# A windowed-attention and expert layer on one core: clearing buffers later, router weights earlier, and the last chunk of rows in another order

## The chip, the core and the metric

The kernel runs on one core of a Trainium2 chip. The metric is device time in microseconds (us), lower is better. The core's engines are TensorE (PE, matrix products, whose weight loads are shown apart as PEld), VectorE (DVE), ScalarE (ACT), GpSimd (POOL) and SyncE (SP). SyncE here only issues DMA transfers. Each engine has its own instruction stream in program order, and they meet at semaphores.

## The reference

The input x is 8 sequences of 512 tokens with 256 channels, in float32. All that follows is float32.

```
xn   = layernorm(x)                                  # per token, eps 1e-5
qkv  = xn @ qkv_w.T                                  # 32 heads of 8
att  = q.k * 8**-0.5 * (8 - |i-j|/2)/8               # only for i-8 <= j < i+8
s    = softmax(att) @ v @ proj_w.T + proj_b
e    = argmax(xn @ router_w), score = sigmoid(max)   # 8 experts, one for each token
f    = (silu(xe @ gate_w[e]) * (xe @ up_w[e])) @ down_w[e]     # xe = xn * score
f   += (silu(xn @ shared_gate_w) * (xn @ shared_up_w)) @ shared_down_w
out  = x + s * silu(f)
```

## The kernel before, in words

The 4096 tokens are 32 tiles `t` of 128. X holds all of x, and later the normalised rows, then rows scaled for the experts, then the attention's result. xnT holds the normalised x transposed, with zero columns at both ends of each sequence. Attention goes by 64 units `n` of 2 blocks of 32 queries. A unit runs over several turns of one main loop, `for n in range(LAST + 1)` with LAST = 66, that each engine has in its own stream:

- PE: `scores(n)` from the block-diagonal key buffer kBD and the query buffer qBD (two of each, taken in turn for each half sequence), then `weighted(n - 2)`, the probabilities times the values in VB, and `output(t)` ("pr"), the projection of a finished tile.
- VectorE: `weigh` (scores times the distance weights into Sx), `largest`, `flipped` (32x32 transposes of the exponentials into PTs), `invert`, `divide`, `turned` (for the normalised output O and OT).
- GpSimd: `banded` (a mask, in some turns) and `subtract`; ACT: `exps`.

Ahead of the loop: SP issues the loads of x in five groups (`GROUPS`: tiles 0 to 3, 4 to 11, 12 to 19, 20 to 27, 28 to 31), and behind the first group those of two sets of constants and of the weights of q, k and v. VectorE takes the moments of group 0 (`moments(0)`, one instruction for each tile), forms mean and deviation in small operations on 128x4 (`variance`, `deviation`, with a square root on ACT), and normalises tiles 0 to 3 (`normalise(0)`; each second tile raises the semaphore `n_xn` by 1). PE transposes them and forms q, two sets of keys and the values of sequence 0. VectorE goes on with the moments of the other 28 tiles, then writes ones into two columns of each part of VB, and waits for the scores of unit 0. Meanwhile GpSimd clears `blank`, the ends of xnT, both kBD, both VB and the three Sx, and makes two bfloat16 copies of constants, all in one run. The semaphore `s_zero` is raised after the ends of xnT (to 1) and after Sx (to 2); ACT's first copy into qBD, VectorE's ones and first `weigh`, and SP's main loop wait for 2. Router weights are the last 8 columns of the tile wqkv; PE's first product for values (`values(0)`) waits for them.

The feed-forward part: the shared expert's products are the jobs "sg", "su" (gate and up, for half of the hidden channels of a sequence) and "sd" (down, for two tiles). ACT copies an "sd" into `shared_rows`. The routed tokens are sorted by expert into DRAM, worked on in tiles between units 18 and 40 or so, and their results lie in `ys_dram`. For each chunk `c` of two tiles (16 chunks), GpSimd's `gather(c)` adds the routed rows to the shared rows by two indirect DMAs, ACT's `silu(c)` takes a tanh, VectorE's `silu(c)` makes f(1 + tanh), VectorE's `result(c)` multiplies 0.5 of that with the attention's result (which `attention(t)` has put into X with the bias added), and GpSimd's `add_out` stores it with addition onto out, where x was copied before. The last chunk is different: `result(15)` adds it to the two tiles of x in XR, and SP stores XR plainly.

All products but scores and weighted values share four PSUM banks psM, given out in turn in the order of the list ORDER, which `jobs_of(n)` fills. `jobs_of(64)` holds "sd" for the last chunk, at U - 3 (U = 64), and "pr" of tile 30; "pr" of tile 31 stands in turn 66. In turn 64 PE does `weighted(62)` first and then that "sd" and "pr".

Of the kernel before, what the change touches and what calls it, by code (L numbers as in the profile page):

```python
# [11 lines left out]
ALU = mybir.AluOpType  # L12
# [3 lines left out]
P = 128  # L16
BATCH, SEQ, C = 8, 512, 256
# [3 lines left out]
T = NTOK // P  # L21
# [7 lines left out]
QB = 32  # L29
# [28 lines left out]
CT = 2  # L58
# [92 lines left out]


def result_at(n):
    last = {NC - 2: U + 1, NC - 1: LAST}
    return [c for c in range(NC) if last.get(c, max(C_STEP + 2 + c * 4 // 3, 4 * c + 6)) == n]


# [4 lines left out]
def build(nc, x, wqkv_d, wproj_d, router_w, gate_w, up_w, down_w, sgate_w, sup_w, sdown_w,  # L162
# [3 lines left out]
    with ctx:  # L166
# [132 lines left out]
        @block.sync  # L299
        def _(sp):  # L300
            for i, (lo, hi) in enumerate(GROUPS):
                sp.dma_start(X[:, lo:hi, :], x_tiles[:, lo:hi, :]).then_inc(s_x[i], 16)
                if i == 0:
                    sp.dma_start(cst[:, :], const[:, 0:C_STAY]).then_inc(s_const, 16)
                    sp.dma_start(rcst[:, :], const[:, C_STAY:C_END]).then_inc(s_const, 16)
                    sp.dma_start(wqkv[:, :, 0:3 * C], wqkv_d.rearrange("(k p) f -> p k f", p=P)).then_inc(s_wq, 16)
            for dst, src in ((wsgu[:, :, 0:F], sgate_w), (wsgu[:, :, F:2 * F], sup_w), (wsdn[:, :, :], sdown_w)):
                sp.dma_start(dst, src.rearrange("(k p) f -> p k f", p=P)).then_inc(s_ws, 16)
            sp.dma_start(wqkv[:, :, 3 * C:], router_w.rearrange("(k p) f -> p k f", p=P)).then_inc(s_wr, 16)
            sp.dma_start(wp[:, :, :], wproj_d).then_inc(s_ws, 16)  # L310
            sp.wait_ge(s_zero, 1)
            v_rows = v_dram.rearrange("(b w) c -> w b c", b=BATCH)
            for lo, hi in ((0, WIN), (WIN + SEQ, PADW)):
                sp.dma_start(v_rows[lo:hi], blank[0:hi - lo, :].unsqueeze(1).broadcast_to([hi - lo, BATCH, C])).then_inc(s_pad, 16)
            sp.wait_ge(s_zero, 2)
            sp.wait_ge(s_one, 1)

            def fill(i):
                n_r = min(4, NT - 4 * i)
                sp.dma_start(xs_dram[i * 4 * P:(i * 4 + n_r) * P, :].rearrange("(p r) c -> p r c", r=n_r),  # L320
                             blank[:, :].unsqueeze(1).broadcast_to([P, n_r, C])).then_inc(s_fill, 16)

            def keep_v(b):
                sp.wait_ge(a_V, BT * (b + 1))
                at = b * PADW + WIN
                sp.dma_start(v_dram[at:at + SEQ, :].rearrange("(t p) c -> p t c", p=P), vS[b % 2][:, :, 0:C]).then_inc(x_vd[b % 2], 16)

            def spread_v(n):
                b = n // UB
                sp.wait_ge(x_vd[b % 2], 16 * (b // 2 + 1))  # L330
                if n == 0:
                    sp.wait_ge(s_pad, 16 * 2)
                if n >= 2:
                    sp.wait_ge(a_PV, n - 1)
                at = first_key(n)
                for h in range(HS):
                    sp.dma_start(VB[n % 2][QB * h:QB * h + QB, :, :, h, 1:1 + VQ].rearrange("p i k c -> p (i k) c"),
                                 v_dram[at:at + P, h * VQ:(h + 1) * VQ].rearrange("(a p) c -> p a c", p=QB)).then_inc(x_v[n % 2], 16)

            def expert(i):  # L340
                return sp.value_load(etabi[0:1, i:i + 1], min_val=0, max_val=E - 1)

            def load_weights(i):
                e = expert(i)
                if i >= 2:
                    full(sp, ("xb", i - 2))
                for w, c0 in ((gate_w, 0), (up_w, F)):
                    sp.dma_start(egu[:, i % 2, :, c0:c0 + F],
                                 w[bass.ds(e, 1)].rearrange("e (k p) f -> p (e k) f", p=P)).then_inc(b_wg[i % 2], 16)

            def load_down(i):
                e = expert(i)
                if i >= 2:
                    full(sp, ("xc", i - 2))
                sp.dma_start(edn[:, i % 2, :, :],
                             down_w[bass.ds(e, 1)].rearrange("e (k p) c -> p (e k) c", p=P)).then_inc(b_wd[i % 2], 16)

            def load_rows(i):
                if i >= 4:
                    full(sp, ("xa", i - 4))  # L360
                sp.dma_start(stage[:, i % 4, :], xs_dram[i * P:(i + 1) * P, :]).then_inc(b_in[i % 4], 16)

            def preset(k):
                rows = slice(k * NTOK // 8, min((k + 1) * NTOK // 8, NTOK - CT * P))
                sp.dma_start(out[rows, :], x[rows, :]).then_inc(d_pre, 16)

            for n in range(LAST + 1):
                if BATCH < n - 1 < U:
                    spread_v(n - 1)
                if ROUTE <= n < ROUTE + 8:  # L370
                    preset(n - ROUTE)
                if n == C_STEP:
                    full(sp, ("xc", NX - 1))
                    sp.dma_start(XR.rearrange("p (t c) -> p t c", t=CT), x_tiles[:, T - CT:T, :]).then_inc(d_x, 16)
                for i in range(2 * n - 4, 2 * n - 2):
                    if 0 <= i < 10:
                        fill(i)
                if n == E0 - 1:
                    for k in range(SENDS):
                        sp.wait_ge(r_scat[k], 16 * (T // SENDS))  # L380
                    sp.wait_ge(r_tab, 1)
                    sp.wait_ge(s_cast, 2)
                    for i in range(2):
                        load_rows(i)
                for i in pair_at(n + 1, 0):
                    if i >= 2:
                        load_rows(i)
                for i in pair_at(n, 1):
                    load_down(i)
                for i in pair_at(n, 0):  # L390
                    load_weights(i)
                if 0 <= n - 1 < BATCH:
                    keep_v(n - 1)
                if 0 <= n - 1 <= BATCH:
                    spread_v(n - 1)
            sp.wait_ge(d_pre, 16 * 8)
            sp.wait_ge(d_o, 1)
            sp.dma_start(out_v[:, T - CT:T, :], XR.rearrange("p (t c) -> p t c", t=CT)).then_inc(d_end, 16)
            sp.wait_ge(d_end, 16)
            for b in range(3):  # L400
                sp.wait_ge(d_st[b], 16 * len(range(b, NC - 1, 3)))

        @block.gpsimd
        def _(pool):
# [1 line left out]
            zero(blank[:, :], 0.0)  # L406
            zero(xnT[:, :, :, 0:WIN], 0.0)
            zero(xnT[:, :, :, WIN + SEQ:PADW], 0.0).then_inc(s_zero, 1)
            for i in range(2):
                zero(kBD[i][:, :, :, :], 0.0)  # L410
            for v in VB:
                zero(v[:, :, :, :, :], 0.0)
            for s in Sx:
# [197 lines left out]
        def _(dve):  # L611
# [98 lines left out]
            def weigh(n):  # L710
                dve.wait_ge(a_S, n + 1)
                if n == 0:
                    dve.wait_ge(s_zero, 2)
                if n >= 3:
                    dve.wait_ge(a_PT, n - 2)
                s = Sx[n % 3][:, :, :].rearrange("p (j g) k -> p j g k", j=KC)[:, :, :, 0:KW]
                tt(s, psS[:, :, 0:BW].rearrange("p j (g k) -> p j g k", k=KW),  # L717
                   mw.unsqueeze(1).unsqueeze(1).broadcast_to([P, 2, G, KW]), ALU.mult).then_inc(a_mul, 1)
# [85 lines left out]
            def result(c):  # L804
# [2 lines left out]
                dve.wait_ge(a_s, CT * c + CT)  # L807
                dve.wait_ge(d_w, c + 1)
                stt(s, shared_rows(t).rearrange("p t c -> p (t c)"), 0.5, s, ALU.mult, ALU.mult).then_inc(d_g, 1)
                if c == NC - 1:  # L810
                    dve.wait_ge(d_x, 16)
                    dve.wait_ge(d_g, c + 1)
                    tt(XR, s, XR, ALU.add).then_inc(d_o, 1)

            moments(0)
            variance(0)
# [1 line left out]
            normalise(0)  # L818
            for i in range(1, len(GROUPS)):
                moments(i)  # L820
            dve.wait_ge(s_zero, 2)
            for v in VB:
                for h in range(HS):
                    for c in (0, 2 * VW - 1):
                        ins = nc.vector.memset(v[QB * h:QB * h + QB, :, :, h, c:c + 1], 1.0)
            ins.then_inc(s_one, 1)
            for n in range(LAST + 1):
                if n < U:
# [35 lines left out]
                if n < BATCH:  # L864
                    logits(n)
                for job in jobs_of(n):
                    if job[0] == "pr":
                        attention(job[1])
                if n == ROUTE - 1:
                    choose()  # L870
                for c in result_at(n):
# [3 lines left out]
        def _(pe):  # L875
# [146 lines left out]
            for n in range(LAST + 1):  # L1022
# [12 lines left out]
                    expert_down(i)  # L1035
                for i in pair_at(n, 1)[:1]:
                    expert_up(i)
                if 0 <= n - 2 < U:
                    weighted(n - 2)
                for i in pair_at(n, 1)[1:]:  # L1040
# [1 line left out]
                for i in pair_at(n, 0)[:1]:  # L1042
                    expert_rows(i)
                for job in jobs_of(n):
                    if job[0] in ("sg", "su", "sd"):
                        shared(*job)
                for i in pair_at(n, 0)[1:]:
                    expert_rows(i)
# [43 lines left out]
```

## Time and profile before

| | |
|---|---|
| median of 3 runs | 595.69 us (592.25, 595.69, 595.95) |
| the profiled execution: its own time | 597.03 us |
| the profiled execution: span | 595.0 us |
| PE busy | 545.0 us (92%) |
| VectorE busy | 440.0 us (74%) |
| ACT, GpSimd busy | 240.7 us (40%), 253.8 us (43%) |
| mean granted clock of PE | 0.979 |

The span goes from the profiled execution's first to its last event; its own time is 2.03 us longer. PE's granted clock is given as a share of 2.4 GHz. Busy time of PE is that of pipelined products and says little about its peak; waits and the chain of work are read from the rows below.

### The profile page before, as it was taken

How to read it: one execution, taken by the hardware profiler on the slowest of the kernel's cores; microseconds unless marked ns; L12 is line 12 of the kernel's file. 1: busy time of each engine (PE TensorE's matmuls, PEld its weight loads, DVE VectorE, ACT ScalarE, POOL GpSimd, SP SyncE). 2: the span in 40 equal slices, each digit the busy share in tenths (PEclk: the TensorE clock that was granted, in tenths of full speed). 3: DMA queues.
4: the chain of work that ended last, by engine and by line, in shares of the span. 5: the costliest groups of instructions: out<-in, count | busy, mean ns of one | idle time of the engine just before them, and what ended most of it. 6: DMA issues, size and time to landing. Idle time of an engine off the chain costs nothing.

```text
span 595.0 us, 10334 instructions
## 1 busy us (share of the span) xinstructions
PE 545.0 (92%) x3302; PEld 472.2 (79%) x3302; DVE 440.0 (74%) x1030; ACT 240.7 (40%) x506; POOL 253.8 (43%) x187
## 2 busy tenths in 40 slices
PE   1989999979998999999999999999999999989773
PEld 1747789858876899988899988899888878876662
DVE  6776867898758566566656656655899999989993
ACT  1464454526553433433443442353434454343210
POOL 7122333128885322322422422222466876966442
PEclk9979999989998999999999999999999999999987
DMA  8624533215634667767566757644233755646423
GB/s 304 210 80 141 190 121 124 90 53 181 193 107 138 198 191 208 209 192 211 158 183 212 213 169 213 203 134 133 62 59 59 99 79 83 89 60 92 60 36 54
DMA packets 106618, 83.17 MB, mean 140 GB/s; under 512 B 42181, under 2 KB 104773, under 8 KB 106437
## 3 DMA queue, kind: packets, MB, share of 16 engines
q1 hardware_dynamic: 90724, 65.07, 37.5%
q0 software_dynamic: 10224, 12.33, 12.5%
q10 hardware_dynamic: 5616, 5.11, 2.5%
q8 instruction: 27, 0.44, 0.3%
q14 instruction: 27, 0.21, 0.1%
HBM read 59.41 MB, written 27.00 MB: 145 GB/s over the span
## 4 chain that ended last, share of the span: by engine, by line
PE 60%; DVE 15%; POOL 8%; issue 5%; ACT 5%; DMA 4%; SPq 1%; ACTq 0%; DVEq 0%
PE psM L1002 11%; PE psV L952 11%; PE psS L927 8%; PE psM L1011 5%; PE psM L979 5%; PE psM L938 4%; PE psM L974 4%; PE psM L902 4%; POOL xnT L453 3%; DMA xnT<-ys_dram,slot 3%; PE psM L907 3%; POOL Sx L443 3%; DVE O L769 3%; PE psM L960 3%; DVE PTs L749 2%
## 5 line engine op out<-in xcount | busy, mean ns | idle before, releaser
L443 POOL TENSOR_TENSOR Sx<-Sx,mx 128x752 f32<-128x752 f32 x64 | 98.8, 1544 | 124.4 <-DVE mx L727 124.1
L952 PE MATMUL psV<-VB,PTs 128*128 128x132 f32 x1024 | 132.3, 281 | 16.5 <-DVE O L769 16.5
L952 PEld LDWEIGHTS psV<-VB,PTs 128*128 128x128 f32 x1024 | 126.2, 191 | 21.4 <-issue 20.0
L437 POOL TENSOR_TENSOR Sx<-Sx,cst 128x752 f32<-128x752 f32 x28 | 47.0, 1677 | 184.1 <-DVE Sx L717 184.1
L927 PE MATMUL psS<-kBD,qBD 128*128 128x188 f32 x512 | 97.8, 323 | 0.2 <-DVE Sx L717 0.2
L927 PEld LDWEIGHTS psS<-kBD,qBD 128*128 128x128 f32 x512 | 84.7, 190 | 9.5 <-issue 2.5
L749 DVE STREAM_TRANSPOSE PTs<-Sx 128x512 f32<-128x512 f32 x128 | 82.9, 685 | 4.2 <-ACT Sx L506 4.1
L717 DVE TENSOR_TENSOR Sx<-psS,cst 128x752 f32<-128x752 f32 x64 | 60.0, 938 | 30.0 <-PE psS L927 29.7
L769 DVE TENSOR_TENSOR O<-psV,rs 32x128 f32<-32x128 f32 x256 | 73.5, 287 | 4.8
L1002 PE MATMUL psM<-xT,EB 128*128 128x128 f32 x624 | 76.5, 276 | 0.2 <-DMA EB<-in_L_ffn_up_w 0.2
L1002 PEld LDWEIGHTS psM<-xT,EB 128*128 128x128 f32 x624 | 73.8, 192 | 2.5 <-ACT qBD L495 1.3
L727 DVE TENSOR_REDUCE mx<-Sx 128x16 f32<-128x752 f32 x64 | 59.6, 931 | 13.0 <-POOL Sx L437 11.7
L506 ACT ACTIVATE Sx<-Sx 128x752 f32<-128x752 f32 x64 | 52.9, 827 | 38.5 <-POOL Sx L443 38.5
L979 PE MATMUL psM<-xnT,wsgu 128*128 128x512 f32 x128 | 63.4, 619 | 2.1 <-DVE ag L785 2.1
L476 ACT ACTIVATE kBD<-psM 32x272 f32<-32x272 f32 x128 | 49.2, 385 | 15.1 <-PE psM L907 13.9
L453 POOL DMA_INDIRECT xnT<-ys_dram,slot x28 | 46.4, 1656 | 13.9 <-ACT xnT L476 7.6
L495 ACT ACTIVATE qBD<-psM,cst 128x512 f32<-128x512 f32 x64 | 38.6, 686 | 22.0 <-PE psM L902 22.0
L536 ACT ACTIVATE et<-psM 128x256 f32<-128x256 f32 x39 | 14.9, 383 | 77.5 <-PE psM L1002 73.9
L734 DVE SCALAR_TENSOR_TENSOR ea<-et,psM 128x256 f32<-128x256 f32 x39 | 16.4, 421 | 36.9 <-ACT et L536 35.9
L979 PEld LDWEIGHTS psM<-xnT,wsgu 128*128 128x128 f32 x128 | 23.1, 200 | 19.1 <-issue 16.7
L1011 PE MATMUL psM<-EB,ehT 128*128 128x256 f32 x156 | 36.9, 379 | 0.0
L907 PE MATMUL psM<-xnT,wqkv 128*128 128x272 f32 x128 | 35.0, 398 | 0.9 <-ACT qBD L495 0.9
(107 smaller groups left out, 686.6 us busy)
## 6 DMA issues: line engine op xcount, KB each, us to landing
EB<-in_L_ffn_gate_w SPq DMA_DIRECT2D x39, 256.0 KB, 3.0
EB<-in_L_ffn_up_w SPq DMA_DIRECT2D x39, 256.0 KB, 3.7
EB<-in_L_ffn_down_w SPq DMA_DIRECT2D x39, 256.0 KB, 3.1
VB<-v_dram SPq DMA_DIRECT2D x256, 32.0 KB
stage<-xs_dram SPq DMA_DIRECT2D x39, 128.0 KB, 2.2
ys_dram<-yb ACTq DMA_DIRECT2D x39, 128.0 KB, 3.2
xs_dram<-blank SPq DMA_DIRECT2D x9, 512.0 KB, 3.2
v_dram<-vS SPq DMA_DIRECT2D x8, 512.0 KB, 3.0
```

The source lines that it names most:

```text
L443: nc.gpsimd.tensor_tensor(s, s, mx[n % 3][:, :].unsqueeze(2).broadcast_to([P, 2 * G, KW]), ALU.subtract).then_inc(a_sub, 1)
L453: pool.indirect_dma_start(shared_rows(c * CT)[:, k, :], None, ys_dram, bass.IndirectOffsetOnAxis(ap=slot[:, t:t + 1], axis=0), compute_op= ...
L506: nc.scalar.activation(s, s, ACT.Exp).then_inc(a_exp, 1)
L717: tt(s, psS[:, :, 0:BW].rearrange("p j (g k) -> p j g k", k=KW), mw.unsqueeze(1).unsqueeze(1).broadcast_to([P, 2, G, KW]), ALU.mult).then_ ...
L727: reduce(mx[n % 3][:, :], Sx[n % 3][:, :, 0:KW], AX, ALU.max).then_inc(a_max, 1)
L749: last = nc.vector.transpose(PTs[n % 2][:, k, :, :, :].rearrange("p j i (r q) -> p (j i r) q", q=QB), Sx[n % 3][:, :, k * QB:(k + 1) * QB])
L769: last = tt(o[rows], v[rows, :, :, HD * h:HD * h + HD], inverse[rows].unsqueeze(3).broadcast_to([QB, KC, 8, HD]), ALU.mult)
L927: last = mm(psS[:, j, i * HS * KW:(i + 1) * HS * KW], qBD[h % 2][:, j, k, :, :].rearrange("p s q -> p (s q)"), kBD[h % 2][:, j, :, k * QB: ...
L952: last = mm(psV[:, j, at:at + HS * VW], PTs[n % 2][:, k, j, i, :], VB[n % 2][:, i, k, :, VW * j:VW * j + VW], start=k == 0, stop=k == 1)
L979: last = mm(ps[:, :], wsgu[:, kc, at:at + P], xnT[:, b, kc, WIN:WIN + SEQ], start=kc == 0, stop=kc == KC - 1)
L1002: last = mm(ps[:, f * P:(f + 1) * P], egu[:, i % 2, kc, f * P:(f + 1) * P], xT[:, i % 2, kc, :], start=kc == 0, stop=kc == KC - 1)
L1011: last = mm(ps[:, 0:C], ehT[:, i % 2, fc, :], edn[:, i % 2, fc, :], start=fc == 0, stop=fc == KC - 1)
```

## The change

- SP: router weights are loaded behind the weights of q, k and v, ahead of x groups 1 to 4, instead of behind the shared expert's weights.
- GpSimd: after the clear of kBD[0] it waits for `n_xn` at 2, that is for the normalised tiles 0 to 3. The clears of kBD[1], VB and Sx and both copies follow. `s_zero` has a new step: 2 after kBD[1], 3 after Sx. VectorE and SP now wait for 3, ACT still for 2.
- VectorE: the ones in VB are written by 8 instructions with two columns each, instead of 16 with one.
- PE: in turn 64 "sd" goes ahead of `weighted(62)`. The order of the banks is the same.
- Last chunk: `attention(30)`, `attention(31)` and `result(15)` are replaced by `last_rows(0)` and `last_rows(1)`, both in turn 66. For each of the two tiles: g = 0.5 w bias; x row += g; g = 0.5 w times the projection in PSUM; x row += g. `step` is an instruction with a wait for its end. SP stores each tile's rows when they are ready.

```
@@ SP
                     sp.dma_start(wqkv[:, :, 0:3 * C], ...).then_inc(s_wq, 16)
+                    sp.dma_start(wqkv[:, :, 3 * C:], router_w.rearrange("(k p) f -> p k f", p=P)).then_inc(s_wr, 16)
             for dst, src in ((wsgu[:, :, 0:F], sgate_w), ...
-            sp.dma_start(wqkv[:, :, 3 * C:], router_w.rearrange("(k p) f -> p k f", p=P)).then_inc(s_wr, 16)
...
-            sp.wait_ge(s_zero, 2)
+            sp.wait_ge(s_zero, 3)
...
-            sp.wait_ge(d_o, 1)
-            sp.dma_start(out_v[:, T - CT:T, :], XR.rearrange("p (t c) -> p t c", t=CT)).then_inc(d_end, 16)
-            sp.wait_ge(d_end, 16)
+            for k in range(CT):
+                sp.wait_ge(d_o, k + 1)
+                sp.dma_start(out_v[:, T - CT + k, :], XR[:, k * C:(k + 1) * C]).then_inc(d_end, 16)
+            sp.wait_ge(d_end, 16 * CT)
@@ GpSimd
-            for i in range(2):
-                zero(kBD[i][:, :, :, :], 0.0)
+            zero(kBD[0][:, :, :, :], 0.0)
+            pool.wait_ge(n_xn, 2)
+            zero(kBD[1][:, :, :, :], 0.0).then_inc(s_zero, 1)
@@ VectorE
-                if c == NC - 1:
+            def last_rows(k):
+                t = T - CT + k
+                w, x_row = shared_rows(T - CT)[:, k, :], XR[:, k * C:(k + 1) * C]
+                g = X[:, t, :]
+                if k == 0:
+                    dve.wait_ge(d_w, NC)
                     dve.wait_ge(d_x, 16)
-                    dve.wait_ge(d_g, c + 1)
-                    tt(XR, s, XR, ALU.add).then_inc(d_o, 1)
+                    dve.wait_ge(r_scat[SENDS - 1], 16 * (T // SENDS))
+                step(stt(g, w, 0.5, bias, ALU.mult, ALU.mult))
+                step(tt(x_row, g, x_row, ALU.add))
+                ps = full(dve, ("pr", t))
+                ins = stt(g, w, 0.5, ps[:, 0:C], ALU.mult, ALU.mult)
+                ins.then_inc(a_s, 1)
+                dve.wait_ge(a_s, t + 1)
+                tt(x_row, g, x_row, ALU.add).then_inc(d_o, 1)
...
-                    for c in (0, 2 * VW - 1):
-                        ins = nc.vector.memset(v[QB * h:QB * h + QB, :, :, h, c:c + 1], 1.0)
+                    ins = nc.vector.memset(v[QB * h:QB * h + QB, :, :, h, 0:2 * VW:2 * VW - 1], 1.0)
...
-                    if job[0] == "pr":
+                    if job[0] == "pr" and job[1] < T - CT:
                         attention(job[1])
+                    if job[0] == "pr" and job[1] == T - 1:
+                        last_rows(0)
+                        last_rows(1)
@@ PE
+                if n == U:
+                    shared("sd", U - 3)
                 if 0 <= n - 2 < U:
                     weighted(n - 2)
...
-                    if job[0] in ("sg", "su", "sd"):
+                    if n < U and job[0] in ("sg", "su", "sd"):
                         shared(*job)
```

## Rows read from the trace of the kernel before

**Rows 1.** The page, the chain that ended last: shares of the span by engine

```profile
PE 60%; DVE 15%; POOL 8%; issue 5%; ACT 5%; DMA 4%; SPq 1%; ACTq 0%; DVEq 0%
```

**Rows 2.** Timeline, VectorE, 5.5 to 13.5: start us, duration us, engine, line, operation

```profile
6.09 1.02 DVE L634 TENSOR_SCALAR mv<-mv 128x4 f32<-128x4 f32 x1
7.16 0.87 DVE L636 TENSOR_SCALAR mv<-mv 128x4 f32<-128x4 f32 x1
...
9.17 0.68 DVE L639 COPY mv<-mv 128x4 f32<-128x4 f32 x1
...
10.34 0.83 DVE L645 TENSOR_TENSOR mv<-mv 128x4 f32<-128x4 f32 x1
...
11.40 0.17 DVE L647 TENSOR_SCALAR mv<-mv 128x4 f32<-128x4 f32 x1
```

**Rows 3.** Timeline, GpSimd, 0 to 12: clears and the longer cast

```profile
1.50 3.76 POOL L410 MEMSET kBD<- 128x2176 f32 x2
5.20 1.90 POOL L412 MEMSET VB<- 128x1056 f32 x2
7.03 2.80 POOL L414 MEMSET Sx<- 128x1024 f32 x3
...
10.02 1.13 POOL L418 CAST maskb<-EB 128x1128 bf16<-128x1128 f32 x1
```

**Rows 4.** Timeline, 565 to 595, all engines

```profile
570.20 2.08 PE L952 MATMUL psV<-VB,PTs 128*128 128x132 f32 x16 [0.35 <-DVE O L769]
...
575.49 3.05 PE L952 MATMUL psV<-VB,PTs 128*128 128x132 f32 x16 [3.21 <-DVE O L769]
...
576.51 1.30 DVE L749 STREAM_TRANSPOSE PTs<-Sx 128x512 f32<-128x512 f32 x2
...
578.34 2.61 PE L974 MATMUL psM<-wsdn,hTs 128*128 128x256 f32 x8
...
580.98 0.60 ACT L476 ACTIVATE xnT<-psM 128x512 f32<-128x512 f32 x1 [4.51 <-PE psM L974]
...
588.14 0.69 DVE L802 SCALAR_TENSOR_TENSOR xnT<-EB,xnT 128x512 f32<-128x512 f32 x1 [2.03 <-ACT EB L551]
588.86 0.42 DVE L796 TENSOR_TENSOR X<-psM,cst 128x256 f32<-128x256 f32 x1
...
590.12 0.69 DVE L813 TENSOR_TENSOR EB<-X,EB 128x512 f32<-128x512 f32 x1
590.88 0.39 SPq L398 DMA_DIRECT2D out<-EB  x1
```

**Rows 5.** Timeline, 0 to 48, all engines; in brackets idle time before, and its releaser

```profile
13.12 9.23 DVE L624 BATCH_NORM_STATS2 stats<-X 128x6 f32<-128x256 f32 x28
...
15.42 3.75 PE L902 MATMUL psM<-xnT,wqkv 128*128 128x256 f32 x8 [0.78 <-ACT xnT L476]
...
21.75 4.14 PE L938 MATMUL psM<-wqkv,xnT 128*128 128x264 f32 x16 [0.28 <-DMA wqkv<-in_L_ffn_router_w]
22.30 0.88 DVE L825 MEMSET VB<- 32x4 f32 x16
...
27.20 0.94 DVE L717 TENSOR_TENSOR Sx<-psS,cst 128x752 f32<-128x752 f32 x1 [4.02 <-PE psS L927]
```

**Rows 6.** View of tile X, 0 to 40: ns min/median/max, first and last start

```profile
L624 DVE BATCH_NORM_STATS2 stats<-X x32: 407/408/427, 4.3 to 21.9; 128x6 f32<-128x256 f32 x32
```

**Rows 7.** DMA issues of 2.2 to 2.6 and of 8.8 to 11.9: us to landing

```profile
wqkv<-in_L_attn_qkv_w SPq DMA_DIRECT2D x1, 768.0 KB, 6.9
...
X<-in_L_attn_x SPq DMA_DIRECT2D x1, 512.0 KB, 10.5
```

**Rows 8.** Timelines, VectorE and GpSimd, 460 to 466: one row of each

```profile
462.58 0.65 DVE L802 SCALAR_TENSOR_TENSOR xnT<-EB,xnT 128x512 f32<-128x512 f32 x1
...
462.17 1.68 POOL L453 DMA_INDIRECT xnT<-ys_dram,slot  x1 [0.17 <-issue]
```

**Rows 9.** Busy times in 36.5:43.5: length, PE, PEld, DVE, ACT, POOL, PE's clock, DMA share, GB/s

```profile
36.50:43.50 7.00, 5.59 (x9) 3.11 (x10) 6.33 (x11) 3.80 (x9) 1.81 (x2) 0.54 0.01 2
```

More of the change, by code:

```diff
@@ L153, in result_at @@
 def result_at(n):
-    last = {NC - 2: U + 1, NC - 1: LAST}
+    last = {NC - 2: U + 1, NC - 1: LAST + 1}
     return [c for c in range(NC) if last.get(c, max(C_STEP + 2 + c * 4 // 3, 4 * c + 6)) == n]
@@ L712, in weigh @@
                 if n == 0:
-                    dve.wait_ge(s_zero, 2)
+                    dve.wait_ge(s_zero, 3)
                 if n >= 3:
@@ L820, in _ @@
                 moments(i)
-            dve.wait_ge(s_zero, 2)
+            dve.wait_ge(s_zero, 3)
             for v in VB:
                 for h in range(HS):
-                    for c in (0, 2 * VW - 1):
-                        ins = nc.vector.memset(v[QB * h:QB * h + QB, :, :, h, c:c + 1], 1.0)
+                    ins = nc.vector.memset(v[QB * h:QB * h + QB, :, :, h, 0:2 * VW:2 * VW - 1], 1.0)
             ins.then_inc(s_one, 1)
```

## The prediction

> **What bounds the kernel now.** I read the chain that ended last first, as shares and then in order of time. PE holds 60% of it and VectorE 15% [rows 1], so the long middle of the kernel is PE's. The diff touches nothing there: it works at the two ends, where PE waits. What the reader is to see is therefore where each end's chain runs, and whether what is won at the start is still there at the end. In between every wait is on another instruction or transfer of the same program, and none on a fixed time, so I carry a shift of the start through whole.
>
> At the start the chain is: first four tiles of x, their moments, the small VectorE operations on 128x4, the four normalisations, PE's transposes, q, keys, values, scores. In the small operations the reader is to see five that take far longer than their shape. A TENSOR_SCALAR of 128x4 took 1.02, and two later ones 0.87 each (the second is not shown, it took 0.88), a COPY 0.68, a TENSOR_TENSOR 0.83; the same TENSOR_SCALAR took 0.17 once GpSimd was quiet [rows 2]. Set beside GpSimd's queue [rows 3] each of them ends where a GpSimd instruction ends: the first at 7.11, where the clear of VB ends (5.20+1.90); the next two with the first and second of the three clears of Sx (0.93 apart from 7.03); the COPY at 9.85, with the last; the TENSOR_TENSOR at 11.17, with the cast (10.02+1.13). VectorE is held by GpSimd.
>
> At the end the chain is: last shared product (sd) on PE, ACT's copy, two gathers that add the experts' rows, tanh, and four VectorE operations, then one store [rows 4]. PE does the weighted values of unit 62 before sd, and stands idle for 3.21 ahead of them, waiting for VectorE's division of unit 61.
>
> **Part 1, the clears.** Removed from the path: 1.02-0.17=0.85, twice 0.87-0.17=0.70, 0.68-0.17=0.51, 0.83-0.17=0.66; together 3.42 [rows 2]. The wait is put after the clear of the first key buffer, and behind it on GpSimd stand that of the second, VB, Sx and both casts. The first clear ends near 3.4 (1.50 plus half of 3.76), before the first of VectorE's long small operations begins at 6.09. The wait is over when the four normalisations end, 0.1 behind the start of the next moments at 13.12 [rows 5]: 13.2-3.4=9.8. Then come 1.88+1.90+2.80=6.6 of clears, to 16.4, and 1.4 of casts, to 17.8 [rows 3]. Who waits for them? ACT's first copies of q and k, now for the second clear only: done at 11.7, before the q product even begins (15.42-3.42=12.0) [rows 5]. VectorE ahead of its writes of ones into VB, and the first weighing: below. GpSimd's own first mask comes after the first weighing. So the move itself costs nothing, with 7 us to spare; without that cover it would cost up to its 6.6. The clears now lie beside the 28 later moments. All 32 moments took 407 to 427 ns, the first four, from 4.3 on, beside a clear of a key buffer, the others beside nothing [rows 6], so I price this at nothing; upper bound, a hold as in rows 2 at each of six clears and casts, 6x0.7=4.2, which would reach the path only past the slack of the next part.
>
> **Part 2, router weights.** PE's first product for values waited 0.28 for them at 21.75 [rows 5]. With everything 3.4 earlier PE would be there at 18.1, and without this edit it would stand there for 3.4+0.28 and the gain would be gone. The edit is thus half of part 1. Issued behind the weights of q, k and v, which landed 6.9 after their issue [rows 7], at 2.3+6.9=9.2, they are there by about 10. The q product needs its weights at 12.0: also there. It adds one issue on SP's queue ahead of four groups of x, and small transfers ahead of theirs. The last of these groups (issued at 8.8 or later, 10.5 to landing) [rows 7] had landed by 21.0, since VectorE took its four moments without idling and ended at 22.35 [rows 5]. If it lands 0 to 0.7 later than that (the router's part is 8 KB; a guess, with the slack below as its test), moments end at 22.4 to 23.1, and the ones (now 8 instructions for 16, so 0.44 for 0.88) end at 22.8 to 23.5. The first weighing was started by PE's scores at 27.20, after 4.02 of idling [rows 5], now 23.8. That holds with 0.3 to 1.0 in hand, and is the tightest cover of the change. What the issues behind it bring, the shared weights and the projection's, PE first uses behind the first scores; they are the same bytes, at most the router's own transfer later. I take 0 for it; bounds 0 and 1.
>
> **Part 3, sd first.** PE is free at 570.20+2.08=572.28; sd at its slow 2.61 ends at 574.9, before the 575.49 at which the weighted values could start anyway [rows 4]. ACT's copy must now wait behind ACT's exponentials of unit 63, which end at 576.5 where the transposes of VectorE start; copy done 577.1. From there to the tanh's end it took 588.14-581.58=6.56 (gathers, landing, tanh), so 583.7 now. This was the end's chain; it is taken away by 4.4. What is late next: VectorE. It was idle for 2.03 before 588.14, so it was through with everything for unit 63 and chunk 14 at 586.11 [rows 4]. That line becomes shorter too: weighted values 62 ran 3.05 at the end of PE's idle stretch against 2.08 for the same sixteen one unit before; with sd in the gap they need not end later than the two transposes, 576.51+1.30=577.81, where VectorE had waited until 578.54. That is 0.73. PE's output product of tile 30, which had queued behind sd until 580.95, follows the division alike. VectorE is free at 586.1-0.7=585.4, or 586.1 if PE stays slow.
>
> **Part 4, row by row.** Removed behind that point: 0.69, 0.42, 0.69, 0.69 with small gaps, from 588.14 to 590.81. Now: the product with tanh 0.69, then eight operations on 128x256. Each is like the 0.42 at 588.86 [rows 4]; with 0.04 at six of the joints 3.6. The first row is stored 1.8 earlier, beside the work on the second; its cost is nothing. Sum: 585.4+0.7+3.6=589.7 at worst, and 589.4 where neighbours overlap as the queue allows; against 590.81 a gain of 1.1 to 1.4, taken 1.3. The chunk's row-wise form by itself costs more VectorE time (3.6 for 2.0); it buys a last store of 128 KB for 256 KB, which I estimate at 0 to 0.5, and take 0.3. From the store's issue to the span's end 4.1 remain. If PE stays slow through both units (0.7 and 1.0 of it) the end gains nothing: bounds -0.4 and +1.9.
>
> GpSimd's accumulating store of chunk 14 now runs beside these operations. In the trace a VectorE operation with both inputs in SBUF took 0.65 wholly inside a gather's 1.68 on GpSimd [rows 8], no more than its usual 0.68, so descriptors cost it nothing. The Trainium skill ("SBUF — State Buffer", Who interferes with whom) has such an operation contend with a GpSimd instruction that reads SBUF; if issuing the store counted as one, the first row would wait for its end, some 1.5 us more. By the trace it does not count.
>
> **The sum.** Profiled execution: span 595.0, time 597.03. 3.42+1.3+0.3=5.0, so span 590.0 and time 592.0. That execution lay 1.34 above the median of the three shown, 595.69, and I take the difference from the median: 590.7.
>
> **Rivals.** (a) The start's shift is lost: the moments end later than the first weighing, or the first mask holds VectorE at another place. Against it: 4.02 of idling. For it: only 0.3 to 1.0 is left of that. All lost, and only the end's 1.6 stay: 594.1. Chance 0.12. (b) The end gives nothing, since PE stays at its slow level and VectorE's line with it: 595.69-3.4=592.3. Chance 0.15. (c) PE's clock is luckier. From 36.5 to 43.5 the granted clock was 0.54, mostly the lower of the levels 1.2 and 2.4 GHz, and PE was busy for 5.59 of it [rows 9]; the same work at the upper level would take 5.59x0.54=3.0, so one such fall costs at most 2.6. A shift by 3.4 may miss it: 588.1. Chance 0.12. (d) The other side: the same mechanism against the change. The fall at the end came with PE's idle 3.21 before unit 62 [rows 4], and PE idles in many places wherever VectorE is late. If the shift turns more of those idles into falls, each takes up to 2.6; two more than before cancel the gain, three make it slower: 590.7+7.8=598.5. Chance 0.06. The Trainium skill ("TensorE: Matmul & The Clock Gate", What's actually happening) says that the monitor's window runs free and does not restart with a kernel, so that a transition's place varies by run; by this rule (c) and (d) change from run to run and a median keeps little of either.
>
> **How the numbers follow.** The forecast itself, 589.5 to 592: 0.55. Rivals as above. Range: from 588.0 (c) to 594.8 (a with the slow clock's ends), leaving out some of (c) and (d). 1%, about what a measurement of this kernel can tell from no change, is 6.0: below 589.7 lies (c), and about a third of the forecast's own spread, 0.12+0.18=0.30, and I give 0.32; above 601.6 only the worst of (d), 0.03.
>
> **What would show it.** The operations on 128x4 all near 0.17 and the normalisations from about 8.4; PE's first transpose near 9.3; no wait for router weights; the first weighing near 23.8 with VectorE idle before it (little idle, or a wait for x at the moments: a). Near the end sd ahead of the weighted values in PE's gap, weighted values 62 in 2.1 and not 3.05 (else b), VectorE without a pause from the product with tanh to the last row. The prediction fails if the stage from 28 to 150 us doesn't run 3.4 earlier throughout, or if the clock rows differ by more than one fall.

## The result, and the profile after

| | kernel before | changed kernel |
|---|---|---|
| median of 7 runs | 593.43 us | 589.39 us |
| range of the runs | 592.12 to 595.95 | 588.57 to 590.37 |
| ratio, 95% interval | | 0.9931 (0.9911 to 0.9951) |
| profiled execution: time, span | 597.03, 595.0 | 589.39, 587.6 |

The change is worth 0.69%, 4.1 us: it lies clear of zero and within 1%. The two profiled executions differ by 7.4, because the one of before was a long one among its runs. A second profile of the kernel before (experiment 8) has a span of 591.5, that is 3.9 more than the changed kernel's, which is nearer to what the runs show.

The start, in the timeline of the changed kernel, all engines (start us, duration us, engine, line, operation; in brackets idle time before it):

```profile
2.74 0.47 SPq L307 DMA_DIRECT2D wqkv<-in_L_ffn_router_w  x1
...
5.95 0.17 DVE L636 TENSOR_SCALAR mv<-mv 128x4 f32<-128x4 f32 x1
...
6.22 0.17 DVE L638 TENSOR_SCALAR mv<-mv 128x4 f32<-128x4 f32 x1
...
6.82 0.17 DVE L641 COPY mv<-mv 128x4 f32<-128x4 f32 x1
...
7.47 0.16 DVE L647 TENSOR_TENSOR mv<-mv 128x4 f32<-128x4 f32 x1
...
8.28 1.38 DVE L654 TENSOR_SCALAR X<-X,mv 128x256 f32<-128x256 f32 x4
...
9.72 1.91 POOL L412 MEMSET kBD<- 128x2176 f32 x1 [6.31 <-DVE X L654]
...
12.38 2.71 DVE L626 BATCH_NORM_STATS2 stats<-X 128x6 f32<-128x256 f32 x8 [2.72 <-DMA X<-in_L_attn_x]
13.41 2.74 POOL L416 MEMSET Sx<- 128x1024 f32 x3
...
17.19 2.00 PE L954 MATMUL psM<-wqkv,xnT 128*128 128x264 f32 x8
...
18.39 4.02 DVE L626 BATCH_NORM_STATS2 stats<-X 128x6 f32<-128x256 f32 x12 [0.29 <-DMA X<-in_L_attn_x]
...
22.35 0.85 DVE L838 MEMSET VB<- 32x8 f32 x8
...
23.56 0.94 DVE L719 TENSOR_TENSOR Sx<-psS,cst 128x752 f32<-128x752 f32 x1 [0.35 <-PE psS L943]
```

The reader is to see that the operations of [rows 2] that GpSimd held take 0.16 to 0.17 now, that GpSimd has been idle for 6.31 before the second clear, and that PE's product for values waits for no load. The first weighing starts at 23.56 for 27.20 [rows 5]. VectorE's cover is all but used up: 2.72 of its idling moved to the moments, where it now waits for x, and only 0.35 are left before the weighing.

The end, from the same timeline:

```profile
566.79 1.89 PE L990 MATMUL psM<-wsdn,hTs 128*128 128x256 f32 x8
...
570.16 2.08 PE L968 MATMUL psV<-VB,PTs 128*128 128x132 f32 x16 [1.48 <-DVE O L771]
...
571.93 1.54 POOL L455 DMA_INDIRECT xnT<-ys_dram,slot  x1 [2.99 <-ACT xnT L478]
571.97 0.73 PEld L976 LDWEIGHTS psM<-wp,OT 128*128 128x128 f32 x4
...
574.20 2.08 PE L968 MATMUL psV<-VB,PTs 128*128 128x132 f32 x16 [1.09 <-DVE O L771]
...
578.66 0.68 DVE L804 SCALAR_TENSOR_TENSOR xnT<-EB,xnT 128x512 f32<-128x512 f32 x1
579.37 0.42 DVE L821 SCALAR_TENSOR_TENSOR X<-xnT,cst 128x256 f32<-128x256 f32 x1
579.55 1.29 POOL L432 DMA_DIRECT2D out<-X  x1 [4.23 <-DVE X L811]
...
581.25 2.02 SPq L399 DMA_DIRECT2D out<-EB  x2
...
582.46 0.42 DVE L827 TENSOR_TENSOR EB<-X,EB 128x256 f32<-128x256 f32 x1
```

The product sd stands in PE's gap, VectorE has no pause before the product with tanh (2.03 before [rows 4]), and the eight operations follow each other to 582.88. From the weighing of unit 63 to VectorE's end it is 17.36 us (565.52 to 582.88) for 19.97 (570.84 to 590.81). But from there to the span's end it is 4.72 for 4.19. That last stretch is what the experiments turned up.

How the lead runs through the kernel: the start of the weighing of unit n (VectorE) in the profile of before, its second profile and the changed kernel's:

| unit | before | before, second profile | changed | lead on the first | lead on the second |
|---|---|---|---|---|---|
| 0 | 27.20 | 26.63 | 23.56 | 3.64 | 3.07 |
| 2 | 47.72 | 45.99 | 42.91 | 4.81 | 3.08 |
| 32 | 336.69 | 334.95 | 332.29 | 4.40 | 2.66 |
| 33 | 351.85 | 349.17 | 347.44 | 4.41 | 1.73 |
| 55 | 521.96 | 519.48 | 517.82 | 4.14 | 1.66 |
| 56 | 529.46 | 525.54 | 523.87 | 5.59 | 1.67 |
| 63 | 570.84 | 567.18 | 565.52 | 5.32 | 1.66 |

### The profile page after: what moved, and what is told of

Its sections match the earlier page's. It is cut to its first block, busy times and chain, and to the rows that moved or that the text cites. A ratio compares the mean times of both kernels' runs of the same rounds, so it can differ in the third digit from the quotient of the medians.

```text
span 587.6 us, 10330 instructions
## 1 busy us (share of the span) xinstructions
PE 541.6 (92%) x3302; PEld 468.8 (80%) x3302; DVE 437.7 (74%) x1026; ACT 240.9 (41%) x506; POOL 254.1 (43%) x187
## 4 chain that ended last, share of the span: by engine, by line
PE 54%; DVE 17%; POOL 11%; issue 5%; DMA 5%; ACT 5%; SPq 1%; ACTq 0%; DVEq 0%
PE psM L1018 11%; PE psV L968 10%; PE psS L943 7%; PE psM L1027 5%; POOL xnT L455 4%; PE psM L995 4%; DMA xnT<-ys_dram,slot 4%; POOL Sx L445 3%; PE psM L954 3%; DVE O L771 3%; PE psM L918 3%; PE psM L990 3%; DVE PTs L751 3%; PE psM L923 2%; PE psM L976 2%
## 5 line engine op out<-in xcount | busy, mean ns | idle before, releaser
L968 PEld LDWEIGHTS psV<-VB,PTs 128*128 128x128 f32 x1024 | 125.3, 190 | 19.9 <-issue 18.6
L995 PE MATMUL psM<-xnT,wsgu 128*128 128x512 f32 x128 | 61.7, 605 | 2.1 <-DVE ag L787 2.1
L976 PE MATMUL psM<-wp,OT 128*128 128x256 f32 x128 | 33.9, 388 | 2.7 <-DVE OT L780 2.0
```

Of the source, the lines that this page charges most:

```text
L968: last = mm(psV[:, j, at:at + HS * VW], PTs[n % 2][:, k, j, i, :], VB[n % 2][:, i, k, :, VW * j:VW * j + VW], start=k == 0, stop=k == 1)
L995: last = mm(ps[:, :], wsgu[:, kc, at:at + P], xnT[:, b, kc, WIN:WIN + SEQ], start=kc == 0, stop=kc == KC - 1)
```

## The experiments

All ratios are against the kernel before on the same chip, with 95% intervals. The letters of the theories and rivals are those of the expectations.

**1. The start alone** (clears, router weights, ones in VB; nothing of the end).

> The start's edits alone (clears behind the first normalisation, router weights sooner, ones in VB by 8 instructions); the end as before. Theory A (both ends are separate, their gains add, and the start's shift is carried to the end): the first weighing starts near 23.6 as in the changed kernel (27.2 before) and the kernel is 3.4 to 3.7 us faster. Rival B (the start's shift is mostly lost in the long middle, and the end makes the whole gain): faster by less than 1 us.

Measured: 0.9936 (0.9912 to 0.996), 3.8 us faster; first weighing at 23.65. That is theory A's case. The whole size of the changed kernel's gain can be had without touching the end, though the interval goes from 2.4 to 5.2. At the end of this profile, in the old order, PE ran at the full clock:

```profile
571.59 2.08 PE L952 MATMUL psV<-VB,PTs 128*128 128x132 f32 x16 [3.21 <-DVE O L770]
...
573.50 1.89 PE L974 MATMUL psM<-wsdn,hTs 128*128 128x256 f32 x8
...
579.90 0.65 DVE L810 SCALAR_TENSOR_TENSOR X<-xnT,X 128x512 f32<-128x512 f32 x1
```

The same two groups of products took 3.05 and 2.61 in the first profile of before [rows 4]; how much of the 3.8 comes from the clock at the end in the other runs isn't shown. Part 3 below comes back to it.

**2. The clears moved, router weights late.**

```diff
+            zero(kBD[0][:, :, :, :], 0.0)
+            pool.wait_ge(n_xn, 2)
+            zero(kBD[1][:, :, :, :], 0.0).then_inc(s_zero, 1)
...
             sp.dma_start(wqkv[:, :, 3 * C:], router_w...)   # where it was
```

> The clears moved, router weights issued late as before. Theory A: PE reaches the first product for values near 18 and waits there until the router weights land at about 21.7, so the first weighing stays near 27 and the kernel gains 0 to 0.3 us. Rival B (PE's scores are reached by another way, the router weights never held them): the first weighing near 23.6 and 3.4 us faster.

Measured: 1.0037 (1.0012 to 1.0061), 2.2 us slower. Rival B falls, and theory A was too kind: the edit by itself harms. Timeline of this kernel:

```profile
21.88 5.44 PE L938 MATMUL psM<-wqkv,xnT 128*128 128x264 f32 x16 [4.63 <-DMA wqkv<-in_L_ffn_router_w]
...
28.63 0.94 DVE L718 TENSOR_TENSOR Sx<-psS,cst 128x752 f32<-128x752 f32 x1 [5.60 <-PE psS L927]
```

PE idles for 4.63 and then takes 5.44 for sixteen products that took 4.14 [rows 5]. All of the 3.4 gained is waited away, and 1.4 more is lost at the first weighing (28.63 for 27.20). The loss is PE's clock: over these products the granted clock was 0.69 (0.50 in their first half), where it was 1.00 over the same products in the kernel before.

**3. The end alone** (sd first, last chunk row by row; start as before).

> The end's edits alone (sd first and the last chunk row by row), the start as before. Theory A: 0.8 to 2.1 us faster; the changed kernel's whole gain of 4.0 less 3.4 to 3.6 for the start leaves about 0.5, its profiled execution by itself shows 2.1 at the end. Rival B (the end makes the whole gain): 3 to 4 us faster.

Measured: 0.9969 (0.9953 to 0.9984), 1.9 us faster, as theory A has it. Alone the two ends give 0.64% and 0.31%, together 0.95% by their sum, where 0.69% was measured; with half-widths of the intervals of 0.15 to 0.24, these agree.

**4 and 5. sd first alone; row by row alone.**

```diff
+                if n == U:
+                    shared("sd", U - 3)
                 if 0 <= n - 2 < U:
                     weighted(n - 2)
```

> Only sd ahead of the weighted values of unit 62; last chunk by the old form. Theory C (the row-wise form costs more VectorE time than its smaller store gives back): 0.5 to 1.5 us faster than the end's edits together, so 1.5 to 3 us faster than before, with VectorE's last operation ending 3 us or more earlier than 590.8. Rival D (my sum: row by row is worth having for its smaller last store): the same as the end's edits together or slower than they.

> Only the last chunk row by row; sd stays behind the weighted values of unit 62. In the profiles so far eight operations on 128x256 follow the product with tanh, 3.5 us from its end to VectorE's last, against 2.0 us by the old form. Theory C (the form costs VectorE time and its early first store gives back little): 0.8 to 1.6 us slower than before. Rival D (it is worth having, or at least free): 0 to 0.5 us faster.

Measured: sd first alone 0.9967 (0.995 to 0.9985), the same as the end's edits together; row by row alone 0.9999 (0.9979 to 1.0018), nothing. So no gain of the row-wise form shows (rival D as I had summed it, a smaller last store), and the 0.8 to 1.6 us that it was to cost (theory C) don't show either. The profiles say why VectorE's time doesn't show. With sd first alone, timeline:

```profile
582.44 0.65 DVE L809 SCALAR_TENSOR_TENSOR X<-xnT,X 128x512 f32<-128x512 f32 x1
...
583.90 1.29 POOL L430 DMA_DIRECT2D out<-X  x1 [4.22 <-DVE X L809]
...
585.28 0.69 DVE L813 TENSOR_TENSOR EB<-X,EB 128x512 f32<-128x512 f32 x1
```

VectorE ends at 585.97, 16.02 after the weighing of unit 63, so 1.2 sooner than in experiment 3 (17.25), and the span ends at 591.8, 5.8 later. Row by row alone VectorE ends at 588.63, and the span only 2.4 later, at 591.0. From VectorE's last operation a plain store thus needs at most 2.4 us to the span's end, and where more passes, something else is late.

**6 and 7. Fewer operations for the rows; one store.**

```diff
+                dve.wait_ge(a_s, t + 1)
+                step(stt(g, w, 0.5, g, ALU.mult, ALU.mult))
+                tt(x_row, g, x_row, ALU.add).then_inc(d_o, 1)
```

(6: `attention(30)` in turn 64, `attention(31)` between the two rows.)

> The whole change, but the projection of tile 30 with its bias is added at its old place in turn 64, where VectorE is idle, and each row then needs a product and an addition behind the product with tanh (tile 31 also its projection): five operations on 128x256 for eight. Theory C: VectorE's last operation ends 1.2 to 1.4 us earlier than in the changed kernel after the same weighing of unit 63, and the kernel is about 1.3 us faster than the changed one, 5 to 5.5 us faster than before. Rival D (PE's product of tile 31 comes too late to use it, or the last store's landing is bound by GpSimd's accumulating store of chunk 14): the same as the changed kernel, 4.0 us faster than before.

> The changed kernel with one last store of 256 KB behind both rows, in place of two of 128 KB. Theory C (the two stores give little): within 0.4 us of the changed kernel. Rival D (the early first store is what pays for the eight operations): 0.5 to 1 us slower than it.

Measured: 0.9925 (0.9906 to 0.9943) and 0.9917 (0.9898 to 0.9936), both like the changed kernel's 0.9931. In 6 VectorE did end 1.3 sooner (16.08 after the weighing of unit 63 for 17.36), and the span ended 6.2 after it for 4.7. Half a store or a whole one, five operations or eight: the span's end doesn't follow them. For the operations it is the profile that says so, for 1.3 us are 0.22%, and the intervals of the two ratios are about 0.2% to either side.

**8. The kernel before once more.**

> The kernel before once more, for a second profile of it. If the extra 1.16 us at unit 2 and 1.45 us at unit 56 by which the profile of the changed kernel pulled ahead are no work of the change, this profile differs from the first one of the same kernel by such steps, at the same or other units. If it agrees with the first profile at every unit, the steps belong to the change.

Span 591.5, time 593.46. The steps at unit 2 (1.16) and at unit 56 (1.44) are in this profile too, so they are none of the change's work. Another thing differs, in the start's timeline:

```profile
5.95 0.25 DVE L634 TENSOR_SCALAR mv<-mv 128x4 f32<-128x4 f32 x1
...
6.24 0.90 DVE L636 TENSOR_SCALAR mv<-mv 128x4 f32<-128x4 f32 x1
...
9.45 0.16 DVE L645 TENSOR_TENSOR mv<-mv 128x4 f32<-128x4 f32 x1
...
10.36 1.94 DVE L652 TENSOR_SCALAR X<-X,mv 128x256 f32<-128x256 f32 x4
```

x landed 0.14 sooner here, the first of the held operations met the change from one clear of VB to the next (0.25 for 1.02), and the cast held the normalisations (1.94 for the four, against 1.38) in place of the small operation of 0.83. Which operations are held, and for how long, hangs on a tenth of a microsecond.

**9 to 12. Is it GpSimd's accumulating store?** By now ten profiles showed the same distance: the span ends 7.6 to 8.3 us after the issue of chunk 14's accumulating store begins on GpSimd, wherever VectorE ended.

```diff
 def result_at(n):
-    last = {NC - 2: U + 1, NC - 1: LAST + 1}
+    last = {NC - 2: U, NC - 1: LAST + 1}
```

(9: this in the kernel before; 10: in the changed one; 11: in that of experiment 6; 12: the changed kernel without this store, so that its output lacks the attention's part of chunk 14.)

> The kernel before, with only result(14) one turn earlier (64 for 65), so that GpSimd issues the accumulating store of chunk 14 right behind the last gather. Theory F (in nine profiles the span ends 7.6 to 8.3 us after the issue of that store begins, while in one where VectorE was late it ended 2.4 us after VectorE's last operation: the end is the later of the two): VectorE's last operation stays within 0.3 us, the span ends 2.4 to 3 us after it and not 4.2, 1.2 to 1.8 us faster. Rival G (the end is VectorE's last operation and a store that takes what it takes, 4.2 us): no change, within 0.3 us.

> The changed kernel with result(14) one turn earlier. Theory F: the product with tanh starts 0.3 us sooner, the span ends 2.4 to 3 us after VectorE's last operation and not 4.7; 1.7 to 2.5 us faster than the changed kernel, 5.5 to 6.5 us faster than before. Rival G: 0.3 us faster than the changed kernel, from the sooner start alone. A third possibility: the earlier store takes DMA time from the last gather, whose landing comes later, and nothing is won.

> As the run before, and the projection of tile 30 added in turn 64, so that five operations on 128x256 follow the product with tanh and not eight. Theory F: now VectorE sets the end, and the 1.3 us that this form saved there without moving the kernel come out: 1 to 1.4 us faster than the run before, 6.5 to 8 us faster than before. Rival G: the same as with the late store.

> The changed kernel without the accumulating store of chunk 14 (its attention part is left out of the output; all else is computed). Theory F: the span ends 2.4 to 3 us after VectorE's last operation and not 4.7, 1.7 to 2.3 us faster than the changed kernel. Rival G (the store is beside the end): no change, within 0.3 us.

| | ratio to before (95%) | store 14 issued | VectorE's end | span's end | from the store | from VectorE's end |
|---|---|---|---|---|---|---|
| before | 1 | 586.92 | 590.81 | 595.0 | 8.1 | 4.2 |
| before, second profile | | 583.27 | 587.14 | 591.5 | 8.2 | 4.4 |
| changed | 0.9931 | 579.55 | 582.88 | 587.6 | 8.1 | 4.7 |
| 1 start alone | 0.9936 | 581.37 | 585.36 | 589.2 | 7.8 | 3.8 |
| 2 clears alone | 1.0037 | 586.16 | 590.10 | 594.0 | 7.8 | 3.9 |
| 3 end alone | 0.9969 | 581.64 | 584.97 | 589.3 | 7.7 | 4.3 |
| 4 sd first | 0.9967 | 583.90 | 585.97 | 591.8 | 7.9 | 5.8 |
| 5 rows alone | 0.9999 | 583.15 | 588.63 | 591.0 | 7.9 | 2.4 |
| 6 fewer operations | 0.9925 | 581.08 | 583.16 | 589.4 | 8.3 | 6.2 |
| 7 one store | 0.9917 | 581.32 | 584.64 | 588.9 | 7.6 | 4.3 |
| 9 before, early 14 | 0.9989 (0.9975 to 1.0004) | 585.02 | 591.26 | 593.9 | 8.9 | 2.6 |
| 10 changed, early 14 | 0.9885 (0.9868 to 0.9902) | 575.63 | 582.77 | 584.9 | 9.3 | 2.1 |
| 11 as 6, early 14 | 0.987 (0.9856 to 0.9884) | 577.75 | 582.62 | 585.6 | 7.9 | 3.0 |
| 12 no store 14 | 0.9884 (0.9868 to 0.9899) | none | 582.93 | 585.1 | | 2.2 |

Theory F stands in 10 and 12, and rival G falls: with the store early or gone the span ends 2.1 to 2.2 after VectorE, and the kernel is 1.15% faster than before, 2.7 us better than the changed one, the intervals apart. In 11 the ratio moved by 0.15% with overlapping intervals, where 1 to 1.4 us had been expected. Counted from the weighing of unit 63, which came 1.6 later than in 10's profile, VectorE ended 1.8 sooner than in 10 (15.7 for 17.4) and the span 0.9 sooner (18.6 for 19.6): the store, issued 7.9 ahead of the end, was in reach again. In 9 the last stretch shrank as expected (2.6 for 4.2), but the gain of 1.2 to 1.8 us that theory F had forecast didn't come: it is 0.6, not clear of zero. In its profiled execution PE was slow (3.86 for the weighted values of unit 62, 3.05 before), and VectorE ended 21.2 after the weighing of unit 63 for 20.0; whether that is so in its other runs isn't shown.

What waits at the very end shows in SP's own waits, once each in the last 30 us. Changed kernel:

```profile
SPq L166 <- PEq L166: 2.6, 1, 2.6
SPq L399 <- DVE EB L827: 1.3, 1, 1.3
SPq L402 <- DMA out<-X: 0.7, 1, 0.7
```

Experiment 10:

```profile
SPq L399 <- DVE EB L827: 1.3, 1, 1.3
SPq L166 <- DMA out<-EB: 1.2, 1, 1.2
SPq L166 <- PEq L166: 0.2, 1, 0.2
```

Line 166 is the closing of the program, where all engines meet. SP waits there for 2.6 in the changed kernel (1.7 and 1.9 in the two profiles of before) and for 0.2 once GpSimd's store is early; 0.2 also in 9 and 12, and 0.4 in experiment 5, where VectorE was late. The row names PE's queue as releaser; PE had long been done, and what was moved was GpSimd's store. Its landing isn't what SP waits for there: that wait (line 402, 0.7) is over when the 2.6 begin. That GpSimd is late at the meeting behind its store is therefore the reading I hold; what it does in that time no row shows.

## Why the prediction was right, point by point

The forecast was 590.7, 5.0 less than before, with a range from 588.0 to 594.8. Measured: 589.39, 4.0 less than the median of before on the same occasion. The base moved down by 2.3 (593.43, where the first three runs gave 595.69), and the gain was 1.0 smaller than forecast. The start was forecast for the right reason; that the end's part came so near is in good part luck, as parts 3 and 4 show.

**Part 1, 3.42 by five held operations: right in kind and size.** All five fell to 0.16 or 0.17. The first weighing came 3.64 sooner than in the first profile and 3.07 sooner than in the second, which had been held differently; the start alone measured 3.8 (2.4 to 5.2). The clears beside the moments cost nothing that shows: eight moments took 2.71 under them, in step with 4.02 for twelve without (0.34 each).

**Part 2, the router weights: right that they are half of the part, wrong in two sizes.** Without them the gain isn't merely gone, the kernel is 2.2 slower; 1.4 of it stands at the first weighing in experiment 2's profile, where PE's clock fell behind the long wait. And the cover was sized too loosely in one step: "the ones (now 8 instructions for 16, so 0.44 for 0.88)". The eight took 0.85. They still ended at 23.20, inside the 22.8 to 23.5 that I gave, and 0.35 of idling was left. VectorE did wait for x at the moments, 2.72 and twice 0.3; I had named such a wait as a sign of rival (a), but the first weighing was still started by PE's scores.

**The shift is carried through the middle: right, with noise.** Between units 2 and 55 the lead stays within 0.7 of itself on the first profile. On the second it falls by 0.93 in one step at unit 33 and to 1.66 in all. Such steps also stand between two profiles of the same kernel, so one pair of profiles can't tell a shift that is lost from one that isn't. Experiment 1's own profile shows how little: its lead on the first profile is 3.55 at unit 0 and 3.90 at unit 63, on the second 2.98 and 0.24. Its runs can tell (2.4 to 5.2 us faster), and rival (a), that most of the start is lost, falls. My own sign, that the prediction fails if the stage from 28 to 150 us doesn't run 3.4 earlier throughout or the clock differs by more than one fall, was badly drawn: from unit 2 on the lead there was 4.8 on the first profile and 3.1 on the second, and against the first the clock differs both at unit 2 and at the end.

**Part 3, sd first: right in direction, but the larger part of what moved is PE's clock.** I gave VectorE's line 0.73, and it moved by 2.05: the multiplication for chunk 14 ended 13.22 after the weighing of unit 63 (578.74) for 15.27 (586.11). The step that failed is "PE's output product of tile 30, which had queued behind sd until 580.95, follows the division alike." It doesn't: its inputs are units 60 and 61, whose division was over, so it runs at once at 572 behind the weighted values of unit 62, and the weighted values of unit 63, which it had held up, start 8.68 after the weighing of unit 63 and not 10.81.

Most of this isn't the order's doing. In the first profile of before PE's granted clock was 0.69 over the weighted values of unit 62 and sd (3.05 and 2.61). In experiments 1, 2 and 5 the order is the old one too, and the clock was 1.00 there (2.08 and 1.89): the weighted values of unit 63 start 9.15 after its weighing, and the multiplication for chunk 14 ends after 13.6. At the same clock the new order is thus worth about 0.4 to VectorE's line, and 1.7 of the 2.05 is the clock's. Of the six profiles with the old order three had the low clock there (the two of before, and 9), of the eight with the new order none. That the new order, which leaves PE 1.48 idle ahead of unit 62 and not 3.21, keeps the clock up would explain why experiments 3 and 4 measured 1.9 and 2.0, but so few profiles don't show it.

**Part 4, row by row: the sum of operations right, the store's price wrong.** From the end of the product with tanh to VectorE's last operation it is 3.54 (forecast 3.6). But "a last store of 128 KB for 256 KB, which I estimate at 0 to 0.5, and take 0.3" and "From the store's issue to the span's end 4.1 remain" took for a store's price what is GpSimd's: with plain stores the end came 2.1 to 2.4 after VectorE (experiments 5, 10 and 12), and one store of 256 KB in place of two of 128 KB changed nothing that shows (7). The last stretch grew from 4.19 to 4.72. I had looked at this accumulating store only as something that might hold VectorE, which it doesn't: two operations of the first row took their 0.42 wholly inside its 1.29. The two errors, +1.3 on VectorE and -0.8 on the store, nearly cancelled: 2.1 in the profile for 1.6 forecast, and 1.9 in the runs of experiment 3. That is luck, the more so as the +1.3 rests on a slow clock in the profile that I had started from.

**Rivals (b) to (d), PE's clock.** The first profile's fall at 36.5 to 43.5 [rows 9] is missing in the changed kernel, whose shared products behind the same idle 2.05 took 1.98:

```profile
34.26 1.98 PE L995 MATMUL psM<-xnT,wsgu 128*128 128x512 f32 x4 [2.05 <-DVE ag L787]
```

But the second profile of the unchanged kernel lacks its cost too (its lead at unit 2 grew by the same 1.16), experiment 4, whose start is unchanged, has it, and so do experiments 6, 11 and 12, whose start is the changed one (3.78 for these products). It is a matter of the execution. The Trainium skill ("TensorE: Matmul & The Clock Gate", What's actually happening) has the monitor's window run free of the kernel, so that the place of a transition varies. The trace agrees: behind the same 2.05 of idling these four products took 1.98 or 1.99 in three of the 14 profiles and 3.2 to 3.8 in the others, with either start. The price at unit 2 was 0.9 to 1.3, not the 2.6 that I gave as the most: the products are on the path for only part of that stretch. At the end (b) didn't come true: sd took 1.89 and the weighted values 2.08. Yet the start alone, with sd in its old place, shows the same 2.08 and 1.89 behind an idle stretch of 3.21, so the full clock there can't be put down to the change for certain.

## What to carry to other kernels

Small vector operations that take 0.7 to 1.0 us where the same one takes 0.17 elsewhere are probably held; lay GpSimd's instructions beside them, move what nobody needs yet behind them, and move with it every load that the gain will run into, for one edit without the other made this kernel slower. Before pricing the end of a kernel as "the last operation and its store", see how long each engine needs behind its own last transfer: with SP's waits in the profile, the closing wait of 1.7 to 2.6 us was there to be read, and moving one multiplication, and with it GpSimd's last store, a turn ahead was worth 2.7 us, where the whole rewriting of the end had measured 1.9. And before a term is read off one profile, see what clock PE had there, and take a second profile of the same kernel: here 1.7 us of the end were the clock's. When a product is put ahead of another, look up which units each product behind it reads.

## What the runs showed of the hardware

- From the issue of GpSimd's last accumulating store of 256 KB to the span's end it took 7.6 to 8.3 us in ten profiles, and 7.9 in an eleventh (experiment 11). Where that store was early or gone, the span ended 2.1 to 2.2 after the last vector operation with SP's plain stores of 128 KB behind it, and 2.6 with one of 256 KB (experiment 9).
- Eight VectorE clears of 32x8 columns took 0.85, sixteen of 32x4 took 0.88: half the instructions, the same time.
- Behind a wait of 4.63 PE took 5.44 for sixteen products (128x264) at a granted clock of 0.69; behind one of 1.94 (experiment 3) it took 3.80 at 1.00.
- Behind the same idle stretch of 3.21, PE's weighted values of unit 62 and sd ran at a granted clock of 1.00 in three profiles (experiments 1, 2 and 5) and of 0.56 to 0.69 in three others (the two of before, and 9).
- Operations on 128x4 that GpSimd's clears held were held until the running GpSimd instruction ended; starting 0.14 sooner freed one of them (0.25 for 1.02).
